# Half of the down products with the tokens streaming, in float32r, in an attention and mixture-of-experts kernel

## The reference

```python
x = x + attention(layernorm(x), ctx_1024)      # 4 x 256 tokens of 128, 1601 keys a batch, scores clipped, softmax
x = x + ffn(layernorm(x))

def ffn(flat):                                 # 1024 tokens, 8 experts, 256 hidden, top 2
    scores = softmax(flat @ router_weight.T + router_bias)
    topk_w, topk_idx = top_k(scores, 2)
    gu = einsum('th,ehn->ten', flat, gate_up_proj) + gate_up_bias
    gate = minimum(gu[..., :256], 7); up = clip(gu[..., 256:], -7, 7)
    act = (up + 1.0) * gate * sigmoid(1.702 * gate)
    down = einsum('tei,eih->teh', act, down_proj) + down_bias
    out = (take(down, topk_idx) * topk_w).sum(axis=1)
```

## Time and profile before

| | |
|---|---|
| median of 3 runs | 156.71 us (156.7 to 156.9) |
| the profiled execution | 156.96 us, of which the span is 155.2 us |
| PE busy | 149.2 us (96%) |
| PEld busy | 136.0 us (88%) |
| DVE busy | 103.2 us (66%) |
| ACT busy | 100.8 us (65%) |
| POOL busy | 49.8 us (32%) |
| granted TensorE clock | full in all 40 slices of the span |

### The profile page before, as it was taken

One profiled execution on the slowest core, in us unless ns is written; L12 is line 12 of the kernel. 1 busy time (PEld: TensorE's weight loads), 2 busy tenths in 40 slices (PEclk: granted clock), 3 DMA queues, 4 the chain that ended last, 5 costly groups with the idle time before them and its releaser, 6 DMA issues.

```text
span 155.2 us, 3023 instructions
## 1 busy us (share of the span) xinstructions
PE 149.2 (96%) x1004; PEld 136.0 (88%) x1004; DVE 103.2 (66%) x288; ACT 100.8 (65%) x205; POOL 49.8 (32%) x49
## 2 busy tenths in 40 slices
PE   7998799999999999999999999999999999999993
PEld 7988699999999999989988888788888888887892
DVE  0668958386859595963683899957654377552773
ACT  3183878657484736468866656957788677779450
POOL 1356529243505300210067643312333321233020
PEclk9999999999999999999999999999999999999999
DMA  4979999700000000000000000000000000000022
GB/s 116 371 292 404 388 401 384 225 1 4 0 2 0 4 0 0 4 0 2 0 0 4 0 0 0 0 4 0 2 0 0 0 0 0 0 4 0 4 68 68
DMA packets 5909, 10.69 MB, mean 69 GB/s; under 512 B 380, under 2 KB 3080, under 8 KB 5896
## 3 DMA queue, kind: packets, MB, share of 16 engines
q1 hardware_dynamic: 4968, 10.00, 17.9%
q10 hardware_dynamic: 928, 0.53, 1.2%
HBM read 10.00 MB, written 0.52 MB: 68 GB/s over the span
## 4 chain that ended last, share of the span: by engine, by line
PE 78%; DVE 10%; POOL 4%; ACT 3%; issue 3%; DVEq 0%
PE T L1147 14%; PE O L1041 13%; PE S L944 11%; PE S L946 10%; PE S L945 10%; PE T L1025 6%; PE S L951 3%; POOL ex L309 2%; DVE xT L847 2%; DVE up L838 1%; PE S L1147 1%; DVE w_lo L779 1%; DVE sc L631 1%; ACT pr L419 1%; POOL rstd L287 1%
## 5 line engine op out<-in xcount | busy, mean ns | idle before, releaser
L838 DVE TENSOR_SCALAR up<-up 128x512 f32<-128x512 f32 x32 | 13.9, 434 | 24.7 <-ACT up L504 24.7
L350 POOL TENSOR_TENSOR x<-x,xn 128x512 f32<-128x512 f32 x13 | 17.3, 1331 | 38.6 <-ACT xn L524 38.6
L427 ACT ACTIVATE pT<-T 128x512 f32<-128x512 f32 (+1 forms) x32 | 15.4, 513 | 18.4 <-PE T L1025 18.4
L524 ACT ACTIVATE xn<-T,w_scaled 128x128 f32<-128x128 f32 x56 | 16.1, 374 | 17.2 <-PE T L1147 14.1
L944 PE MATMUL S<-x_hi,w_hi 128*128 128x512 f32 x64 | 26.8, 419 | 0.2 <-DVE w_lo L779 0.2
L1041 PE MATMUL O<-pT,ctx_sb 128*128 128x128 f32 (+1 forms) x208 | 25.9, 275 | 0.2 <-ACT pT L427 0.2
L945 PE MATMUL S<-x_lo,w_hi 128*128 128x512 f32 x64 | 25.3, 395 | 0.0
L946 PE MATMUL S<-x_hi,w_lo 128*128 128x512 f32 x64 | 25.3, 395 | 0.0
L1041 PEld LDWEIGHTS O<-pT,ctx_sb 128*128 128x128 f32 (+1 forms) x208 | 24.6, 192 | 0.6 <-ACT pT L427 0.5
L631 DVE TENSOR_SCALAR_CACHE_REDUCE sc<-S,clip_hi 128x400 f32<-128x400 f32 (+1 forms) x32 | 18.9, 630 | 8.7 <-PE S L946 8.5
L498 ACT ACTIVATE keysT_sb<-S,gate_bias 128x512 f32<-128x512 f32 x32 | 22.7, 708 | 1.7 <-PE S L946 1.6
(11 more groups left out here) (127 smaller groups left out, 248.4 us busy)
## 6 DMA issues: line engine op xcount, KB each, us to landing
keysT_sb<-in_ctxT SPq DMA_DIRECT2D x3, 801.0 KB, 9.9
ctx_sb<-in_ctx SPq DMA_DIRECT2D x3, 768.0 KB
gu_sb<-in_gu SPq DMA_DIRECT2D x1, 2048.0 KB, 14.9
ctx_sb<-in_ctx SPq DMA_DIRECT2D x3, 256.0 KB, 4.5
x_sb<-in_x ACTq DMA_DIRECT2D x1, 384.0 KB, 5.0
keysT_sb<-in_ctxT SPq DMA_DIRECT2D x1, 289.0 KB, 5.5
out_x<-xn SPq DMA_DIRECT2D x1, 256.0 KB, 2.3
out_x<-xn SPq DMA_DIRECT2D x2, 128.0 KB, 1.8
```

Of the source, the lines that this page charges most:

```text
L350: nc.gpsimd.tensor_tensor(acc, acc, y_sb[:, k % 2, :], ALU.add).then_inc(y_added, 1)
L524: ins = nc.scalar.activation(y_sb[:, k % 2, t * DIM:(t + 1) * DIM], T[k % 2][:, t * DIM:(t + 1) * DIM], ACT.Copy, scale=w_scaled[:, bass.d ...
L838: nc.vector.tensor_scalar(up[:, k % 2, ih, :], up[:, k % 2, ih, :], 2.0 * LIMIT, 1.0 - LIMIT, ALU.min, ALU.add).then_inc(up_clipped, 1)
```

## The change

For the steps k = 0 and 1 (first half of the tokens) the down product is turned: the down weights are stationary and 512 tokens of activations stream, in three float32r products for each inner half (`down_turned`). It needs high and low parts of both. ScalarE makes the high part of the activations (`act_high`, a copy) and of the pair's down weights (`down_high`), GpSimd the low parts (`act_low`, two a step; `down_low`, one a pair). They lie in tiles that the attention part has left: `ct_hi`, `ct_lo`, and `g_hi`, `g_lo` for the weights.

The result has the tokens on the free axis, so a token's weight must stand in every partition: the routing weights `wT` go to DRAM (`w_rows`) and come back broadcast to all partitions. VectorE weights the result (`weight_yT`, which takes the place of `scale_y` for these steps) and GpSimd adds it into `yT`. At the end `turn_back` adds the bias products and the turned `yT` in the bank O, before the last two down products; ScalarE copies O, and GpSimd adds it to `x1`. For k = 2 and 3 nothing changes but the order around them. `transpose_x2(last)` now stands before the down product of step 0; the bias products of the first half stand in `turn_back`.

```diff
+        act_hi, act_lo = ct_hi, ct_lo
+        dn_hi, dn_lo = g_hi[:, 0:4 * DIM], g_lo[:, 0:4 * DIM]
+        w_first = ctx_sb[0][:].rearrange("p t d -> p (t d)")[:, 0:2 * HTOK]
+        w_rest = sc[:].rearrange("p b k -> p (b k)")[:, 0:(EXPERTS - 2) * HTOK]
+        yT = ctx_sb[1][:].rearrange("p t d -> p (t d)")[:, 0:HTOK]
...
+            sp.wait_ge(wT_copied, 1)
+            sp.dma_start(w_rows, wT[:, 0:HTOK]).then_inc(w_rows_out, 16)
+            sp.wait_ge(o_done, 1)
+            sp.wait_ge(p_ready, TILES)
+            sp.wait_ge(w_rows_out, 16)
+            sp.dma_start(w_first, w_rows[0:2].rearrange("e t -> (e t)").partition_broadcast(P)).then_inc(w_first_in, 16)
+            sp.dma_start(w_rest, w_rows[2:EXPERTS].rearrange("e t -> (e t)").partition_broadcast(P)).then_inc(w_rest_in, 16)
...
+            def act_low(i, k):
+                j = i * 2 + k
+                for ih in range(2):
+                    pool.wait_ge(act_hi_ready, j * 2 + ih + 1)
+                    nc.gpsimd.tensor_tensor(act_lo[k][:, ih * HTOK:(ih + 1) * HTOK], act_t[k][:, ih, :],
+                                            act_hi[k][:, ih * HTOK:(ih + 1) * HTOK].bitcast(F32),
+                                            ALU.subtract).then_inc(act_lo_ready, 1)
+            def down_low(i):
+                nc.gpsimd.tensor_tensor(dn_lo, dn_sb[:, bass.ds(i * (4 * DIM), 4 * DIM)], dn_hi.bitcast(F32),
+                                        ALU.subtract).then_inc(dn_lo_ready, 1)
+            def add_expert(i, k):
+                _, h = PAIR_STEPS[k]
+                if h == 0:
+                    pool.wait_ge(yT_weighted, i * 2 + k + 1)
+                    acc = yT
+                else:
+                    pool.wait_ge(y_scaled, i * 2 + k - 1)
+                    acc = x1[:, HALF:TILES, :].rearrange("p t d -> p (t d)")
+                if k or not isinstance(i, int) or i:
+                    pool.wait_ge(y_added, i * 4 + k)
+                else:
+                    pool.wait_ge(yT_blank, 1)
+                nc.gpsimd.tensor_tensor(acc, acc, y_sb[:, k % 2, :], ALU.add).then_inc(y_added, 1)
+            pool.wait_ge(o_done, 2)
+            nc.gpsimd.memset(yT, 0.0).then_inc(yT_blank, 1)
+            pool.wait_ge(dn_hi_ready, 1)
+            down_low(0)
+            act_low(0, 0)
             root2(3)
-            for b in range(HALF // TPB, BATCHES):
-                router_exponentials(b)
-            def add_expert(step, k):
-                _, h = PAIR_STEPS[k]
-                pool.wait_ge(y_scaled, step + 1)
-                acc = x1[:, h * HALF:(h + 1) * HALF, :].rearrange("p t d -> p (t d)")
-                if not isinstance(step, int) or step >= 1:
-                    pool.wait_ge(y_added, step)
-                nc.gpsimd.tensor_tensor(acc, acc, y_sb[:, k % 2, :], ALU.add).then_inc(y_added, 1)
-            for k in range(4):
-                add_expert(k, k)
+            router_exponentials(2)
+            act_low(0, 1)
+            router_exponentials(3)
+            add_expert(0, 0)
+            add_expert(0, 1)
+            add_expert(0, 2)
+            down_low(1)
             with pool.Fori(1, PAIRS - 1) as i:
-                for k in range(4):
-                    add_expert(i * 4 + k, k)
-            add_expert((PAIRS - 1) * 4, 0)
-            pool.wait_ge(y_scaled, STEPS - 2)
-            pool.wait_ge(bias_added, 1)
+                act_low(i, 0)
+                add_expert(i - 1, 3)
+                act_low(i, 1)
+                add_expert(i, 0)
+                add_expert(i, 1)
+                add_expert(i, 2)
+                down_low(i + 1)
+            i = PAIRS - 1
+            act_low(i, 0)
+            add_expert(i - 1, 3)
+            act_low(i, 1)
+            add_expert(i, 0)
+            add_expert(i, 1)
+            pool.wait_ge(half0_copied, 1)
             nc.gpsimd.tensor_tensor(out_sb[:, 0:HALF, :].rearrange("p t d -> p (t d)"),
-                                    x1[:, 0:HALF, :].rearrange("p t d -> p (t d)"), y_sb[:, 1, :],
+                                    x1[:, 0:HALF, :].rearrange("p t d -> p (t d)"), y_sb[:, 0, :],
...
+            def act_high(i, k, ih):
+                act.wait_ge(act_ready, (i * 4 + k) * 2 + ih + 1)
+                nc.scalar.activation(act_hi[k][:, ih * HTOK:(ih + 1) * HTOK], act_t[k][:, ih, :],
+                                     ACT.Copy).then_inc(act_hi_ready, 1)
+            def down_high(i):
+                nc.scalar.activation(dn_hi, dn_sb[:, bass.ds(i * (4 * DIM), 4 * DIM)], ACT.Copy).then_inc(dn_hi_ready, 1)
...
-            expert(1, 1, 4)
+            act_high(0, 0, 0)
+            silus(1, 1, 4, 0)
+            ups(1, 1, 4, 0)
+            silus(1, 1, 4, 1)
+            act_high(0, 0, 1)
+            split_x2(last)
             copy_wT(0)
-            split_x2(last)
-            for k in range(4):
-                e, h = PAIR_STEPS[k]
-                act.wait_ge(route_ready, h + 1)
-                scale_y(k, k, e)
-                s = k + 2
-                e, h = PAIR_STEPS[s % 4]
-                expert(s, s % 4, (s // 4 * 2 + e) * 4)
-            with act.Fori(1, PAIRS - 1) as i:
-                for k in range(4):
-                    scale_y(i * 4 + k, k, i * 2 + PAIR_STEPS[k][0])
-                    s = k + 2
-                    e, h = PAIR_STEPS[s % 4]
-                    expert(i * 4 + s, s % 4, i * 8 + (s // 4 * 2 + e) * 4)
+            ups(1, 1, 4, 1)
+            act_high(0, 1, 0)
+            act_high(0, 1, 1)
+            with act.Fori(0, PAIRS - 1) as i:
+                expert(i * 4 + 2, 2, i * 8 + 0)
+                expert(i * 4 + 3, 3, i * 8 + 4)
+                act.wait_ge(route_ready, 2)
+                scale_y(i, 2, lambda: down_high(i + 1))
+                expert(i * 4 + 4, 0, i * 8 + 8)
+                act_high(i + 1, 0, 0)
+                act_high(i + 1, 0, 1)
+                scale_y(i, 3)
+                expert(i * 4 + 5, 1, i * 8 + 12)
+                act_high(i + 1, 1, 0)
+                act_high(i + 1, 1, 1)
+            copy_wT(1)
             i = PAIRS - 1
-            for k in range(4):
-                if k < 2:
-                    scale_y(i * 4 + k, k, i * 2 + PAIR_STEPS[k][0])
-                if k == 0:
-                    copy_wT(1)
-                s = k + 2
-                if s < 4:
-                    expert(i * 4 + s, s, (i * 2 + PAIR_STEPS[s][0]) * 4)
+            expert(i * 4 + 2, 2, i * 8)
+            expert(i * 4 + 3, 3, i * 8 + 4)
+            act.wait_ge(half0_done, 1)
+            nc.scalar.activation(y_sb[:, 0, :], BIAS[0][:], ACT.Copy).then_inc(half0_copied, 1)
...
+            def weight_yT(i, k):
+                step = i * 4 + k
+                dve.wait_ge(y_done, step + 1)
+                if isinstance(i, int) and i == 0:
+                    dve.wait_ge(w_first_in, 16)
+                    weights = w_first[:, k * HTOK:(k + 1) * HTOK]
+                else:
+                    dve.wait_ge(w_rest_in, 16)
+                    dve.wait_ge(y_added, step - 1)
+                    weights = w_rest[:, bass.ds(i * (2 * HTOK) + (k - 2) * HTOK, HTOK)]
+                nc.vector.scalar_tensor_tensor(y_sb[:, k % 2, :], T[k % 2][:], 1.0 / ALPHA, weights,
+                                               ALU.mult, ALU.mult).then_inc(yT_weighted, 1)
+            def expert(i, k, split=False):
+                step = i * 4 + k
                 clip_ups(step, k, 0)
                 product(step, k, 0)
                 clip_ups(step, k, 1)
-                if split is not None:
-                    split_w_hi(split, k % 2, step + 1)
+                if split:
+                    split_w_hi(i * 2 + k, k % 2, step + 1)
                 product(step, k, 1)
-                if split is not None:
-                    split_w_lo(split, k % 2)
+                if k == 1 or k == 2:
+                    weight_yT(i, k - 1)
+                if split:
+                    split_w_lo(i * 2 + k, k % 2)
...
-            residual_moments(last)
+            add_router_bias(last - 1)
+            residual_stats(last)
+            logit_maximum(last - 1)
+            residual_mean(last)
+            logit_differences(last - 1)
+            residual_variance(last)
             clip_ups(0, 0, 1)
             product(0, 0, 1)
             normalise(xn2, x1, mv2, rstd2, last * TPB, TPB, rstd2_ready, BATCHES, xn2_ready)
-            add_router_bias(last - 1)
-            logit_maximum(last - 1)
-            logit_differences(last - 1)
+            split_x2(last)
             clip_ups(1, 1, 0)
             product(1, 1, 0)
             clip_ups(1, 1, 1)
-            split_x2(last)
             product(1, 1, 1)
...
+            def down_turned(i, k):
+                step = i * 4 + k
+                if isinstance(i, int) and i == 0:
+                    pe.wait_ge(t_free[k], T_TOTAL[k])
                 else:
-                    pe.wait_ge(y_scaled, step - 1)
+                    pe.wait_ge(y_scaled, i * 2 + k - 1)
```

(53 more changed lines are left out.)

65 lines of the change are left out of this document (34 added, 31 removed).

## The result

The changed kernel takes **174.41 us** (median of 4 runs, 174.31 to 174.54), the kernel before 156.75 in the same measurement: a ratio of 1.113 (1.111 to 1.115), 17.7 us more. The forecast was 171.1 us, 161.5 to 178. The profiled execution has a span of 172.7 us, 17.5 over the 155.2 of before.

What follows compares the result with a forecast made beforehand. TensorE bounds the kernel before; changed, it waits for GpSimd and VectorE. Stalls of 17.9, less 1.3 already waited and 2.2 of saved work, give +14.4: 171.1 us, range 161.5 to 178.

Steps and rivals of the forecast that it cites:

- the exclusion: VectorE and GpSimd operations block each other, except short powers and VectorE work with one operand in PSUM.
- rival (a): Blocking between VectorE and GpSimd costs little and only the order counts: +3.8, 160.5 us; chance 0.14.
- The beginning: TensorE loses 3.5 us before the last transposes of xn2, 2.3 before down(2), 1.0 before down(3).
- Pair 1: Blocked VectorE operations, then copy and act_low, hold down(4) for 2.6 and down(5) for 1.4: 4.0 us.
- Steady stall before down(7), down(11): 2.2 each: TensorE waits 2.2 us at each for VectorE's last product, delayed by the add, w_hi copy and down_low.
- the walk: Operation-by-operation timing from the start of the preceding down product; add's input scaled at 3.45, last product ending at 6.95.
- A product beside act_low: Sign of being right: products and w_lo of 1.5 us and more next to act_low.
- The end: TensorE waits 1.2 us before the turning back and 0.5 before the last bias products: 1.7 us.
- 8 x 0.111 = 0.9: Turning the result back adds four products of 128 columns, costing TensorE 0.9 us.
- rival (c): TensorE's clock falls during stalls, slowing matmuls after those above 2 us, 2 to 3 us each: 180; chance 0.04.
- A clock below 1: Sign of being wrong: TensorE's granted clock falls below 1.00 (2.4 GHz).
- Hidden: Row write and weight broadcasts through memory, down_high in ScalarE's free time and the new first output cost no time.

Runs made afterwards that it cites:

- run 5: Changed kernel with GpSimd's sums of the first half and low parts of the down weights replaced by equally long five-column powers, both left out: 164.47 us.
- run 1: Changed kernel with GpSimd's root of the last batch between the two act_low of step 0 instead of behind both: 173.35 us.
- Runs 4 and 5: The first of them: changed kernel with each act_low replaced by a six-column power on GpSimd, low parts left out: 174.37 us. The other is run 5.
- run 10: Changed kernel with ScalarE's copy of the second weighting matrix (wT) ahead of the last roundings instead of behind them: 176.83 us.
- runs 8 and 9: The first is experiment 8; the second is that kernel with the turning back's four bias products first, then the four turned ones: 158.88 us.
- run 2: Changed kernel with 13 unread products filling TensorE's wait before the last transposes of xn2: 173.86 us.
- experiment 8: Changed kernel with the turned products in plain float32, no split of activations or down weights: 160.8 us, ratio 1.023 to the kernel before.

## Why the prediction was right, and where it was not

**Sign, size and mechanism: right.** The time is in the range and 3.3 us over the point. The chain of waits gives TensorE 46% of the span where it had 78%, and run 5 shows that the exclusion read from the earlier trace rows makes up 9.9 us of it; the forecast had 10.6, the distance from rival (a), that it costs little (160.5 us), to its 171.1. Rival (a) falls with that run and with the result.

**The beginning: right.** 3.5 forecast and 3.50 measured, 2.3 and 1.81 (start of down(2) less the start of the matmul before, less 0.234), 1.0 and 0.87. The sum of them holds; as separate prices they don't add (run 1: taking away 2.8 of the first gains 1.1).

**Pair 1: 4.0 forecast, 3.6 measured**, 2.3 in the turned product of step 4 and 1.3 in that of 5.

**"Steady stall before down(7), down(11): 2.2 each": wrong in place.** Neither waits. In the walk, the add of step 6 is issued ahead of w_hi and the last product of step 7, and blocks them; in the trace its scaled input comes 0.55 later than in the walk (4.00 us after down(6) instead of 3.45), and VectorE has begun that product at 122.40, 0.15 before the add. The four scalings and the copy take 1.66 us; the walk's 3.45 leaves them that much only if they begin as TensorE ends the down product, at 1.78. They begin 2.34 after its start, and in the kernel before it was 2.09 (112.24 after 110.15), which could have been read there:
```profile
112.24 1.14 ACT L524 ACTIVATE xn<-T,w_scaled 128x128 f32<-128x128 f32 x4 [1.11 <-PE T L1147]
```
```profile
120.73 0.37 ACT L577 ACTIVATE xn<-T,w_scaled 128x128 f32<-128x128 f32 x1 [1.36 <-PE T L1248]
...
121.52 0.87 ACT L577 ACTIVATE xn<-T,w_scaled 128x128 f32<-128x128 f32 x3
```
Add and low part of the weights then fall on w_lo and the clip of step 8. The time lost moves to steps 8 and 9; the pair comes to 20.97 against 20.8. That so many exclusive operations lose about as much wherever they meet is argued, not shown; that the pair agrees to 0.2 us is in part luck, as it hides one wrong step.

**"A product beside act_low" as the sign to look for: wrong.** Runs 4 and 5 tell the nine operations of a pair apart: sums and low weights block VectorE, the four low parts of the activations do so for some 0.5 us. They cost by their length, in the series product, rounding, low part, sixth matmul, and in the queue ahead of root and exponentials.

**The end: 1.7 forecast, 2.3 measured, in other places.** Nothing before the turning back (its 1.2 was there in run 10, as 1.68, once TensorE came earlier), 1.4 for wT instead of 0.5, 0.9 for the low part of step 12.

**What the sum lacked.** Turning back +1.3: "8 x 0.111 = 0.9" and "the bias products only move" took each product at its price in a row; alternating, they cost 3.2 instead of 2.0 (runs 8 and 9). And the clock: +1.4 in A and +1.7 in D, which is rival (c) at a third of the size that I gave it. With the waits of stretch D 1.6 us shorter than forecast (2.3 against 1.7 + 2.2) these terms make 2.8 of the 3.1 that A and D lack. A clock below 1 was one of the signs of being wrong, and it came. I had it as all or nothing with a chance of 0.04, partly on a misreading: before the change TensorE does wait over 0.6 us, 0.64 us at 17.84 and 1.12 at the very start, though never near 3. It belonged into the sum wherever a stall of several us was forecast, at least as a term of the range. But run 2 shows that such a term counts little where a wait for another engine follows.

**Hidden: right.** The 1.5 MB broadcast took 8.7 us and the 0.5 MB one 5.4, against an estimate of 3.6 for the latter, and nobody waits for either; the rounding with both sides in SBUF took 0.63, against 0.60.

## What to carry to other kernels

Before work is moved onto GpSimd to relieve TensorE, count how many operations of each kind will meet on GpSimd and VectorE with no operand in PSUM, and what stands behind them in GpSimd's queue; here 3.0 us of saved matmuls (by the forecast's spacing) cost 16.6 to feed, the 13.6 of experiment 8 and these 3.0. A stall taken away is worth its length only if the wait behind it has another cause. And keep products with few rows together instead of alternating them with full ones.
